# Banded attention: the mask multiply of key tiles 0 and 4 of each group is issued by GpSimd, the other six stay on VectorE

## The reference, cut to what matters

```python
def local_gqa_attn(x, wq, wk, wv, wo):
    ...
    k, v = (repeat_kv(k), repeat_kv(v))
    i = jnp.arange(x.shape[1])
    diff = i[:, None] - i[None, :]
    mask = (diff >= 0) & (diff < WIN)          # WIN = 32
    return merge_heads(sdpa(q, k, v, mask)) @ wo
```

## Time and profile before

| | us |
|---|---|
| median of 3 runs | 1845.2 (1843.34 to 1852.63) |
| the profiled execution | 1845.48 |
| its span, first to last instruction | 1843.4 |
| banded stage, from the first exp to the last values | 1555.8 to 1623.9 |
| TensorE busy over the span | 1620.1 (88%) |
| VectorE busy | 1018.0 (55%) |
| ScalarE busy | 817.5 (44%) |
| GpSimd busy | 328.1 (18%) |

### The profile page before, as it was taken

How to read it: one execution, slowest core, us unless ns; L and a number is a source line. 1 busy time by engine, 2 the same in 40 slices (tenths; PEclk the granted TensorE clock), 3 DMA queues, 4 the chain that set the end, 5 groups by cost and what they waited for, 6 DMA issues and landing times. The chain is left out here.

```text
span 1843.4 us, 24909 instructions
## 1 busy us (share of the span) xinstructions
PE 1620.1 (88%) x8725; PEld 870.6 (47%) x8725; DVE 1018.0 (55%) x2284; ACT 817.5 (44%) x1322; POOL 328.1 (18%) x459
## 2 busy tenths in 40 slices
PE   6588985899998996899789989998599985979998
PEld 2325653344443564445544555666333333555665
DVE  6775338878783334634563443455733447964544
ACT  4253334366675432333233343222688865753221
POOL 1104331322232422300330023000100100023000
PEclk9798997799999998999889999999799987989999
DMA  4633115201000411000000004553221013214553
GB/s 103 255 69 149 54 36 143 75 28 54 27 28 2 156 50 42 1 1 1 1 0 1 1 30 102 125 120 80 75 75 33 17 37 111 76 31 102 129 115 92
DMA packets 56076, 121.00 MB, mean 66 GB/s; under 512 B 8423, under 2 KB 34695, under 8 KB 51155
## 3 DMA queue, kind: packets, MB, share of 16 engines
q1 hardware_dynamic: 53484, 114.34, 23.0%
q0 software_dynamic: 2432, 5.00, 0.8%
q10 hardware_dynamic: 39, 0.07, 0.0%
HBM read 86.17 MB, written 19.96 MB: 58 GB/s over the span
## 5 line engine op out<-in xcount | busy, mean ns | idle before, releaser
L2043 DVE TENSOR_REDUCE a_most<-psum 128x1 f32<-128x512 f32 (+3 forms) x304 | 181.7, 654 | 31.0 <-PE psum L1889 20.2
L2001 ACT ACTIVATE a_probs<-psum 128x512 f32<-128x512 f32 (+1 forms) x304 | 155.4, 577 | 94.8 <-PE psum L1919 94.3
L2874 ACT ACTIVATE t_silu<-psum 128x512 f32<-128x512 f32 x136 | 81.2, 597 | 244.6 <-PE psum L2932 243.5
L2949 PEld LDWEIGHTS psum<-t_slot,t_hid 128*128 128x128 f32 x1024 | 132.6, 192 | 57.8 <-issue 49.8
L2302 ACT ACTIVATE ga_probs<-psum 128x1024 f32<-128x1024 f32 (+2 forms) x160 | 138.5, 950 | 24.1 <-PE psum L2216 23.7
L3045 DVE TENSOR_TENSOR t_prod<-t_silu,psum 128x512 f32<-128x512 f32 x104 | 71.4, 687 | 140.2 <-ACT t_silu L2874 140.2
L2949 PE MATMUL psum<-t_slot,t_hid 128*128 128x128 f32 x1024 | 135.1, 277 | 4.8 <-DVE t_hid L3036 4.8
L2932 PE MATMUL psum<-xnT,t_slot 128*128 128x512 f32 x256 | 132.3, 599 | 3.1 <-ACT t_silu L2874 3.1
L2937 PE MATMUL psum<-xnT,t_slot 128*128 128x512 f32 x256 | 130.9, 593 | 0.0
L1886 PE MATMUL psum<-a_ks,a_qs 96*128 96x512 bf16 (+3 forms) x384 | 120.2, 345 | 4.6 <-DVE a_most L2043 2.9
L1919 PE MATMUL psum<-a_qs,a_ks 128*128 128x512 bf16 (+3 forms) x384 | 110.2, 328 | 5.8 <-DMA a_qs<-a_most_parts 3.2
(11 more groups left out here) (434 smaller groups left out, 3005.8 us busy)
## 6 DMA issues: line engine op xcount, KB each, us to landing
t_spread<-factors SPq DMA_DIRECT2D x64, 512.0 KB, 6.4
m_experts<-experts_dram SPq DMA_DIRECT2D x14, 768.0 KB, 9.8
c_halves<-xnT SPq DMA_DIRECT2D x48, 128.0 KB, 2.3
t_slot<-experts_dram SPq DMA_DIRECT2D x32, 192.0 KB, 5.3
a_qs<-scratch_q SPq DMA_DIRECT2D x16, 288.0 KB
a_ks<-scratch_k SPq DMA_DIRECT2D x24, 192.0 KB
ga_qs<-scratch_q SPq DMA_DIRECT2D x16, 288.0 KB
la_qs<-scratch_q SPq DMA_DIRECT2D x16, 288.0 KB
```

Of the source, the lines that this page charges most:

```text
L2001: act.activation(probs[:, (n * BLOCKS + b) % PROBS, h0:h0 + heads, 0:wide], src, ACT.Exp, scale=SCALE).then_inc(probs_ready, 1)
L2043: v.tensor_reduce(most[:, row, h0:h0 + heads, qt % KPH], src, AX.X, ALU.max).then_inc(max_read, 1)
L2949: ins = pe.matmul(core.psum[:, c, t * P:(t + 1) * P], left[:, t * P:(t + 1) * P], weights, start=pair < 0 and t == 0, stop=False, skip_gro ...
```

## The change

The mask of kt 0 and kt 4 of each group (16 of 64 multiplies, both 128 x 640) is issued by GpSimd with the same operands. It has a semaphore of its own, `masked_g`, for which `values` of these two key tiles wait. GpSimd's copy into `la_vslot` for group n + 1 now stands after the mask of kt 4 of group n in its queue; before, all eight copies stood in a row. VectorE keeps six masks a group; in groups 1 to 4 its residual add, which stood behind the mask of kt 4, now follows the normalisation that is issued after kt 3. TensorE's and ScalarE's instructions and their order stay the same.

```diff
+        masked_g = core.sem(ctx, tag + "masked_g")
...
+        def by_gpsimd(kt):
+            return kt % KPH == 0
+
+        def masks_of(n, kt):
+
+            own = [by_gpsimd(k) == by_gpsimd(kt) for k in range(KT)]
+            return n * sum(own) + sum(own[:kt + 1])
+
+        def keep_band(eng, n, kt, done):
+            wide = width(kt)
+            eng.wait_ge(probs_ready, n * KT + kt + 1)
+            part = probs[:, (n * KT + kt) % PROBS, :, 0:wide]
+            eng.tensor_tensor(part, part, keep[:, 0:wide].unsqueeze(1).broadcast_to([P, G, wide]), ALU.mult).then_inc(done, 1)
...
-            for n in range(GROUPS):
+
+            def values_in(n):
...
+            values_in(0)
+            g.wait_ge(keep_ready, 1)
+            for n in range(GROUPS):
+                for kt in range(KT):
+                    if by_gpsimd(kt):
+                        keep_band(g, n, kt, masked_g)
+                    if kt == KPH + 1 and n + 1 < GROUPS:
+                        values_in(n + 1)
...
             def values(n, kt):
-                pe.wait_ge(masked, n * KT + kt + 1)
+                pe.wait_ge(masked_g if by_gpsimd(kt) else masked, masks_of(n, kt))
...
                 for kt in range(KT):
-                    wide = width(kt)
-                    v.wait_ge(probs_ready, n * KT + kt + 1)
-                    part = probs[:, (n * KT + kt) % PROBS, :, 0:wide]
-                    v.tensor_tensor(part, part, keep[:, 0:wide].unsqueeze(1).broadcast_to([P, G, wide]), ALU.mult).then_inc(masked, 1)
+                    if not by_gpsimd(kt):
+                        keep_band(v, n, kt, masked)
                     if n in range(1, NC + 1) and kt == KPH:
```

## The result

| | before | changed |
|---|---|---|
| median, us | 1844.28 (1843.34 to 1852.63, 4 runs) | 1856.45 (1853.91 to 1861.11, 4 runs) |
| ratio, 95% interval | | 1.0049 (1.0031 to 1.0068) |
| the same, repeated | 1846.89 (1840.76 to 1852.51, 23 runs) | 1858.01 (1857.27 to 1862.03, 6 runs), ratio 1.0067 (1.0044 to 1.009) |
| profiled execution, its span | 1845.48, 1843.4 | 1853.91, 1851.5 |
| banded stage, start of the first exp to start of the last `values` | 1555.84 to 1623.43: 67.59 | 1552.47 to 1629.32: 76.84 |

The changed kernel is slower by 12.2 us between the medians and by 11.1 in the repeat. The ratios on record are 0.49% and 0.67% above 1 (the quotients of the medians 0.66% and 0.60%): a small loss, but both intervals leave 1 out. The stage shows it far more sharply, with 9.25 us on 67.59.

The account below looks back on a forecast made before the run. The prediction took the loop from exp over its mask to `values` to bound the kernel. Pieces of 1.0, 4.6, 1.3, 3.1 and 0.7 us, together 10.7, on 1845.2 gave 1855.9 us, range 1850.5 to 1861.0.

Parts of the forecast that it names:

- the loop: Banded stage, from exp over its mask to `values` at kt 0 and 4: a group takes 9.33 us instead of 7.79.
- GpSimd's price, 1.54: GpSimd's 128x640 mask multiply, priced from its 128x512 multiply and 16x128 subtraction: 1.54 us, bounds 1.27 and 1.85.
- The ways: Delays around GpSimd's mask: 0.07 us from exp to GpSimd, 0.13 from GpSimd to `values`, 1.74 in all with the mask.
- The add: Residual add in groups 1 to 4 collides with GpSimd's mask of kt 4: 0.49 us more, 9.82 a group.
- The exclusion: VectorE and GpSimd multiplies exclude each other; masks of kt 1 and 5 end 0.68 us after GpSimd's, costing nothing, cover 0.13.
- Without it the sum would be 2.0 us smaller: Without the rule that two-input VectorE instructions and GpSimd instructions reading SBUF exclude each other, the sum loses 2.0 us.
- Rival 3: VectorE's queue is the bound, GpSimd's latency hidden: groups fall to 7.38 to 7.46, 4.5 us saved, 1840.7; chance 0.04.
- The sum over the stage: Banded stage, groups 0 to 7: 1.0, 4.6, 1.3, 3.1 and 0.7 us, together 10.7 us longer.
- The other stages as before.: Expected sign: stages outside the banded one stay unchanged, adding nothing to the sum.

Follow-up runs that it names:

- lag three: Changed kernel with `values` three key tiles behind the scores instead of two, ScalarE's two copies one tile later: stage 64.82 us, one execution 1852.74.
- The multiply on a spare tile: Changed kernel, masks of kt 0 and 4 left out, GpSimd multiplying a spare tile that TensorE doesn't wait for: stage 73.93 us, one execution 1852.12.
- the fill: Changed kernel, masks of kt 0 and 4 left out, `values` waiting for GpSimd to fill a spare tile instead: stage 74.20 us, one execution 1859.98.
- the masks left out: Changed kernel without the masks of kt 0 and 4, their `values` waiting only for the exp: stage 65.61 us, one execution 1852.58.
- the third kernel of the last table: Kernel before with `values` three tiles behind, ScalarE's first copy one tile later, residual add after kt 6's mask: 1845.93 us, ratio 0.9994, stage 63.41.
- Lag three alone: Kernel before with `values` three key tiles behind the scores instead of two, both copies one tile later: 1843.32 us, ratio 0.9985.
- the half masks: Changed kernel with masks of kt 0 and 4 split, heads 0 and 1 on VectorE, 2 and 3 on GpSimd: stage 72.75 us, one execution 1854.54.
- The late add: Changed kernel with VectorE's residual add two masks later, after the mask of kt 6: stage 74.87 us, one execution 1858.56.

## Why the prediction was right, and where its steps were off

Forecast were 1855.9 us and a range of 1850.5 to 1861.0; the medians are 1856.45 and 1858.01. The mechanism held: the two crossings of the loop carry the loss. That the total came within 1 us is in part luck. The stage was forecast 1.45 us too dear (points 3 and 7), 2.2 to 2.8 us behind it were not forecast at all (point 8), and the two errors nearly cancel. Step by step:

1. **The loop.** Right. TensorE waits twice a group for GpSimd, 0.94 and 0.58 us, forecast 0.7 to 0.9. Taking the cover's shortage away (lag three) takes the loss away while the other costs nearly stay; the latency by itself brings it back to 9.15.
2. **GpSimd's price, 1.54.** Right within a hundredth in 13 of 16 masks. The prediction's own line gave 1.55, and it went on with 1.54 without a reason; either would have done. The estimate of 1.41 from the Trainium skill, GPSIMD Engine Reference, section 3.1, was too low by 0.13 here. The straight line between the trace's own 0.418 and 1.268 was the better source; undisturbed 320 columns took 0.86, where it gives 0.84.
3. **The ways.** Exp to GpSimd 0.08, where the earlier trace rows has 0.07. GpSimd to `values` 0.055, not 0.13: this was the mis-sized term. The 0.13 came from a single row of another stage, and that row shows no wait in front of its matmul. The row of before ahead of it is TensorE's own work, up to 438.55, so 0.13 was an upper bound:

```profile
438.17 0.38 PE L1919 MATMUL psum<-a_qs,a_ks 128*128 128x128 bf16 x4
```

   The VectorE mask of kt 0 in the loop itself had 0.06 and would have been the better guide. From exp to `values` that makes 1.67 instead of 1.74; 15 crossings x 0.07 = 1.1 us too much. With 1.67 the half loops are 4.64 and 4.55 (measured 4.65 and 4.55), and groups 5 and 6 come to 9.19 (measured 9.20 and 9.19, forecast 9.33).
4. **The add.** Right in size and nearly in reason: 0.49 forecast, 0.46 by undoing it. It starts 0.08 ahead of GpSimd in groups 1 to 3, forecast 0.04. In group 4 it comes 0.19 behind GpSimd; the add then took 1.89 us, the mask of kt 5 came late and `values` of kt 5 waited 0.51 for VectorE. The group took 9.78. Either order costs about the same, as said. In groups 1 to 3 the mask of kt 5 takes 1.93, over the 1.3 to 1.6 that the prediction named.
5. **The exclusion at the masks of kt 1 and 5, forecast as "Nothing; the cover is 0.13 us".** True of the sum, since the cover held (in group 5 `values` 5 start 0.11 us after the end of their mask, which leaves 0.06), but the reading was too mild. The multiply on a spare tile shows that the exclusion alone makes 9.15 / 9.01, and the fill shows that the latency alone makes 9.15 / 9.15. The loss is decided twice, by two paths whose groups differ by less than 0.2 us. "Without it the sum would be 2.0 us smaller" stands (the add's part: 3 x 0.46 + the 0.58 of group 4 = 2.0). What the prediction had not seen is the converse: had `values` not had to wait for GpSimd's multiply at all, its hold on VectorE's next masks would still have cost most of the loss (1.22 of 1.41 us in groups 5 and 6).
6. **Rival 3** falls. The reading beside it, that VectorE looks fullest, was only half true: in the earlier trace rows it holds for the group with the add (7.57 against TensorE's 7.46), not for the one without it (7.11 against 7.38). The rival gave 7.38 to 7.46 us a group if the latency were hidden; with the masks left out the groups stay at 7.79. Its floor was read from TensorE's busy time, but in the order of lag two TensorE also loses 0.27 behind a normalisation and some 0.1 between its instructions.
7. **The sum over the stage.** Forecast +10.7, measured 76.84 - 67.59 = +9.25. By pieces, measured against forecast: up to group 1 +0.56 (1.0), groups 1 to 3 +4.13 (4.6), group 4 +1.27 (1.3), groups 5 and 6 +2.81 (3.1), group 7 +0.49 (0.7). The first piece has a gain in it that the prediction put at nothing. In the kernel before, the first mask of group 0 waited 1.76 us after its exp, until VectorE was through with `LastSplit`:

```profile
1557.09 1.29 DVE L1437 TENSOR_TENSOR la_rest<-la_rest,la_parts 128x512 f32<-128x512 f32 x2 [1.65 <-ACT la_parts L1430]
1558.30 2.35 DVE L2583 TENSOR_TENSOR la_probs<-la_probs,la_keep 128x640 f32<-128x640 f32 x3
```

   GpSimd starts it 0.15 us after its exp, and the way from the first exp to exp 4 is 0.33 us shorter. With the 1.1 of point 3 this is nearly the overshoot of 1.45.
8. **"The other stages as before."** Wrong, and it hid the error of the sum. Behind the last `values` the changed kernel needs 222.17 us in its first profile and 222.80 in the repeat, before 220.01: +2.2 and +2.8. 9.25 + 2.2 = 11.4 is near the difference of the medians (12.2), and 9.33 + 2.8 = 12.1 near that of the repeat (11.1).

The last point needs its rows. First the changed kernel, from its last `values` to the end of the banded stage and then a stretch of an expert stage, 1673.0 to 1676.4:

```profile
core 0: us, PE busy (x) PEld busy (x) DVE busy (x) ACT busy (x) POOL busy (x), PEclk, DMA share, GB/s
1629.30:1636.50 7.20, 5.70 (x39) 4.85 (x40) 0.97 (x4) 2.98 (x5) 0.00 (x0) 0.76 0.00 0
1673.00:1676.40 3.40, 3.40 (x11) 2.32 (x10) 1.91 (x3) 0.00 (x0) 0.00 (x0) 0.51 0.00 0
```

and the same two places in the kernel before:

```profile
1623.40:1629.50 6.10, 4.33 (x39) 3.55 (x40) 1.03 (x5) 2.78 (x5) 0.00 (x0) 1.00 0.00 0
1665.50:1668.90 3.40, 3.40 (x13) 1.63 (x12) 1.92 (x3) 0.00 (x0) 0.00 (x0) 1.00 0.00 0
```

The same 39 matmuls take 5.70 us instead of 4.33, at a mean clock of 0.76: within this stretch the granted clock is 1.2 GHz from 1632.1 to 1635.5, behind groups in which TensorE was busy for 7.44 of 9.20. The tail is 7.22 us from the last `values` to the first residual add, before 6.03. The second dip follows 41 us later. The repeat shows both. It is tempting to put this down to TensorE's waits in the groups, and for the changed kernel nothing contradicts it. But the third kernel of the last table, with no mask on GpSimd and TensorE busy for 7.45 of 7.60 us, shows both dips as well:

```profile
1626.20:1629.60 3.40, 3.33 (x16) 2.99 (x17) 0.00 (x0) 1.60 (x3) 0.00 (x0) 0.51 0.00 0
1667.00:1670.40 3.40, 3.40 (x11) 2.33 (x10) 1.92 (x3) 0.00 (x0) 0.00 (x0) 0.53 0.00 0
```

and needs 222.14 us behind the stage; so does the kernel with the masks left out (221.93), whose groups 5 and 6 are as long as before's. Lag three alone, the half masks and the spare multiply have neither dip (219.94, 220.05 and 220.32). The others lie between. The late add, the fill and lag three with GpSimd's masks show the second dip alone (221.13, 221.40 and 220.66), their tails as short as before's; only kt 0 by GpSimd, and kt 3 and 7 by GpSimd, show neither and still need 220.88 and 220.94. So 1.2 of the 2.2 to 2.8 us lie in the tail and go with the lower clock there. The rest is measured but not split up, and what decides whether the clock falls stays open: I made no run in which the groups were held fixed and the tail changed.

In a single execution the stages ahead count too. The changed kernel's first profile enters the stage 3.4 us earlier than before's, the repeat 2.3 later; the first is why its execution took only 8.4 us more than the profiled one of before, while the medians differ by 12.2.

## What to carry to other kernels

Busy shares made VectorE look like the engine to relieve, but the gain of taking work off it was nil in the groups without the residual add (7.79 with the masks and without) and 0.49 us in those with it, and the new engine's latency fell on the loop from exp to `values` in full. Before moving work to an idle engine, measure the time from producer to consumer for exactly the instructions that move: with less cover than the slower engine's extra time, move others (kt 3 and 7 cost 1.9 us, not 9.3) or add cover first. And see which neighbours run beside the moved work: two multiplies with both inputs in SBUF, one on VectorE and one on GpSimd, ran one after the other here, so that the move relieved VectorE of 1.64 us and put some 1.3 us back into its next masks. Where the cover is short, a larger lag may be the change to make by itself; it was the only one here that gained (0.9985, interval 0.9973 to 0.9998).

## What the hardware showed that I had not expected

- GpSimd releases TensorE as quickly as VectorE does: 0.055 us from the end of the multiply to the matmul, against 0.054 (unrounded times, kt 0 of group 5).
- An instruction of VectorE that is held ends its own length less about 0.14 us behind the holder: the 128x640 mask 0.68 us after GpSimd's (alone 0.82), the residual add of group 4 0.54 after it (alone 0.68). So only about 0.14 us of it ran under the other's.
- GpSimd's 128x512 multiply took 1.36 at its shortest in this stage, with kt 3 and 7 moved, against 1.268 in the earlier trace rows. It was held by a mask of VectorE that was still running. These are the rows, VectorE's first:

```profile
1609.04 0.83 DVE L2440 TENSOR_TENSOR la_probs<-la_probs,la_keep 128x640 f32<-128x640 f32 x1 [0.38 <-ACT la_probs L2572]
```

```profile
1609.64 1.36 POOL L2440 TENSOR_TENSOR la_probs<-la_probs,la_keep 128x512 f32<-128x512 f32 x1 [1.66 <-ACT la_probs L2572]
```

  It starts 0.23 us before the end of that mask. If it is held for this less the 0.12 of the prediction, it would take an estimated 1.25 alone.
- TensorE's clock fell to 1.2 GHz at two places behind the changed code, in kernels whose groups had little in common; where both places show it, 1.9 to 2.8 us more pass behind the stage.
